# Radial layers of the second edge stage: one block-diagonal product of 512 columns instead of four 64-column products of 256

## The chip, the core and the metric

The kernel runs on one core of one Trainium2 chip. The metric is the device time of one execution, in microseconds (us). It is told as the median of several runs.

## The reference

Two graph layers are applied to 2000 nodes of 256 features, with 64000 edges sorted by their target node. The change lies in the edge part of the second layer, cut here to what matters:

```python
r = silu(edge_rbf @ M1)            # edge_rbf 64000 x 16, M1 16 x 64
r = silu(r @ M2)                   # 64 x 64
r = silu(r @ M3)                   # 64 x 64
tpw = (r @ M4).reshape(-1, 4, 64)  # 64 x 256
x0, x1 = up0[src], up1[src]
m0e = tpw[:, 0] * x0 * sh0 + tpw[:, 3] * (x1 . sh1) / sqrt(3)
m1e = tpw[:, 1] * x0 * sh1 + tpw[:, 2] * x1 * sh0
msg0, msg1 = segment_sum(m0e, dst), segment_sum(m1e, dst)
```

The first three lines are the three radial layers. Everything is in float32.

## The kernel before, in words

The program has three parts: the first layer's edge stage (to about 975 us of the trace), the second layer's edge stage (about 975 to 2050 us), and a dense end (node updates, norms, a feed-forward block). No scheduler orders the work. Each engine has its own instruction list, written out by hand, and they meet through semaphores.

The second edge stage goes over the edges in *quads* of 4 x 128 = 512 edges, 126 of them (`NQ`), and in *octets* of two quads, 63 of them (`NO`). The lists are unrolled. Per quad:

- POOL gathers 4 x 128 rows of the node table (`utab`) into `G1`, three quads deep (L423); it waits until DVE has used the slot (`s_prod`).
- PE computes `weights` (L936): the last radial product with M4, four products of 64 rows, 128 columns of weights and 256 moving columns, into banks 2 and 3. There is one such buffer, so it waits for DVE's products of the quad before.
- DVE forms the messages in three products of `weights` and the gathered rows (L1354 once, L1356 twice).
- PE sums them by target node in `segment` (L944, four products side by side of 32 weight columns and 512 moving columns, bank 4). ACT collects the bank (L580 to L582), PE turns it with five small products in `turn` (L954), and DVE adds it to the result two quads late (L1346, four times).

Per octet of 1024 edges the three radial layers run once. `layer` on PE (L923) makes the products of one layer, and `silu` on ACT (L572) applies the activation from PSUM into `R1`, `R2` or `R3`. There are 3 x 63 + 4 = 193 layers. An octet's edges lie in `RBF` and in `R1` to `R3` as two halves of 64 partitions (16 for `RBF`) by 512 columns. A layer has four products: `h` chooses the 64 rows of weights and input, `g` the 256 input columns and the 64 output partitions; output goes to bank `h`, columns 0 to 255. So each uses one quarter of the 128 x 128 array, and `two(w)` stores a layer's matrix twice, one under the other, in the same 64 columns. A float32 product stands in the trace as two records, so a layer has eight matrix records.

PE's order in one octet is: weights (second quad), layer 1, segment, [mix1], layer 2, turn, weights (first quad of the next octet), layer 0, segment, [mix1], turn. `mix1` (L968, L975) is dense work of the attention block, put in during the first 112 quads. SP loads `RBF` (L389), two DMAs of 16 rows an octet, three octets deep. A layer waits for the silu of the layer before it (`s_silu`), a silu for its layer (`s_mlp`).

Of the kernel before, what the change touches and what calls it, by code (L numbers as in the profile page):

```python
# [32 lines left out]
ACT = mybir.ActivationFunctionType  # L33
AX = mybir.AxisListType

P = 128
# [7 lines left out]
H = 64  # L44
# [19 lines left out]
RBS = ROUNDS + 1  # L64
OCT = 8 * P
# [23 lines left out]
def build(nc, A, out):  # L89
    ctx = ExitStack()  # L90
    with ctx:
# [3 lines left out]
        def sem(name):  # L95
            return ctx.enter_context(nc.semaphore(name))
# [17 lines left out]
        ps = ctx.enter_context(nc.psum_tensor("ps", [P, 8, 512], F32))  # L114
# [97 lines left out]
        m1 = a2.take(P)  # L212
        m2 = a2.take(P)
        m3 = a2.take(P)
# [21 lines left out]
        R1 = a3b.take(OCT // 2)  # L236
        R2 = a3b.take(OCT // 2)
        R3 = a3b.take(OCT // 2)
        RBF = a3b.take(3 * OCT // 2).rearrange("p (g e) -> p g e", g=3)
# [48 lines left out]
        rbl = [sem(f"rbl{k}") for k in range(3)]  # L288
# [26 lines left out]
        def _(sp):  # L315
# [66 lines left out]
            with sp.Fori(0, npass) as j:  # L382
                sp.wait_ge(S["s_mlp"], j * MLPS + 9)
                sp.sem_inc(S["s_step"], 1)
                with sp.Fori(0, RBS) as i:
                    for k in range(3):
                        sp.wait_ge(S["s_mlp"], j * MLPS + 9 * i + 3 * k + 1)
                        for h in range(2):
                            sp.dma_start(RBF[h * H:h * H + 16, k, :],  # L389
                                         A["rbf"][bass.ds((3 * i + k) * 32 + 16 * h, 16), :]).then_inc(rbl[k], 16)  # L390
                for k in range(3):
                    sp.wait_ge(rbl[k], (j + 1) * RBS * 32)
                    sp.sem_inc(S["s_step"], 1)
            sp.wait_ge(S["s_base1"], 1)
            ld(fw1.rearrange("p k c -> p (k c)"), A["fw1"], "s_fw1")
# [34 lines left out]
        def _(act):  # L430
# [138 lines left out]
            def silu(j, o, layer_):  # L569

                act.wait_ge(S["s_mlp"], j * MLPS + 3 * o + layer_ + 10)
                act.activation((R1, R2, R3)[layer_].rearrange("p (b e) -> p b e", b=2), ps[:, 0:2, 0:256],  # L572
                               ACT.Silu).then_inc(S["s_silu"], 1)

            def collect(j, n, par):

# [73 lines left out]
            for i in range(8):  # L650
                c, o = divmod(i, 2)
# [5 lines left out]
            for i in range(8):  # L657
                c, k = divmod(i, 2)
# [17 lines left out]
        def _(pe):  # L676
# [30 lines left out]
            for c in range(4):  # L707
                pe.wait_ge(S["s_lt"], 2)
                for k in range(2):
                    mm = pe.matmul(ps[0:H, c, :], w1g[:, k, :], LT[:, k, 512 * c:512 * c + 512],  # L710
                                   start=(k == 0), stop=(k == 1))
# [134 lines left out]
            with pe.Fori(0, npass) as j:  # L846
                for n in range(-3, QT + 6):
# [7 lines left out]
                    b, k = divmod(n - 8, QB)  # L855
# [10 lines left out]
            for c in range(4):  # L866
                pe.matmul(ps[half_of(c), c, 0:NCH], idd, vacc[:, c * NCH:(c + 1) * NCH],
                          start=True, stop=True).then_inc(S["s_u"], 1)
            for i in range(8):
                c, o = divmod(i, 2)  # L870
                pe.wait_ge(S["s_ue"], c + 1)
                if i >= 4:
                    pe.wait_ge(S["s_o0"], i - 3)
                pe.matmul(ps[:, 4 + i % 4, 0:NCH], w2g[half_of(c), o * P:(o + 1) * P], U[half_of(c), c * NCH:(c + 1) * NCH],
                          start=True, stop=True).then_inc(S["s_mo"], 1)
            to_rows(1)
            to_cols(1)
            for i in range(8):
                c, o = divmod(i, 2)
                pe.wait_ge(col[1], 2 * c + 2)  # L880
                pe.wait_ge(S["s_ff"], i - 3) if i >= 4 else pe.wait_ge(row[1], 8)
                for k in range(2):
                    mm = pe.matmul(ps[:, 4 + i % 4, :], wfT[:, k, o * P:(o + 1) * P], YT[:, k, 512 * c:512 * c + 512],
                                   start=(k == 0), stop=(k == 1))
# [6 lines left out]
            for i in range(NT // 2):  # L891
# [3 lines left out]
                for t in range(2):  # L895
                    for k in range(2):
                        mm = pe.matmul(ps[:, 4 + i % 4, t * D + k * P:t * D + (k + 1) * P],
                                       YT[:, k, (2 * i + t) * P:(2 * i + t + 1) * P], bu[:, k, :], start=True, stop=True)
# [11 lines left out]
            def layer(j, o, layer_, par=0, rbn=0, after=True):  # L910

                if layer_ == 0:
                    pe.wait_ge(rbl[par], (j * RBS + rbn + 1) * 32)
                    w, x, k = m1, RBF[:, par, :], 16
                else:
                    w, x, k = ((m2, R1, H), (m3, R2, H))[layer_ - 1]
                if after:
                    pe.wait_ge(S["s_silu"], j * MLPS + 3 * o + layer_)
                pe.sem_inc(S["s_step"], 1)
                for h in range(2):  # L920
                    for g in range(2):
                        hs = slice(h * H, h * H + k)
                        mm = pe.matmul(ps[g * H:(g + 1) * H, h, 0:256], w[hs, 0:H], x[hs, g * 256:(g + 1) * 256],  # L923
                                       start=True, stop=True)
                mm.then_inc(S["s_mlp"], 1)

            def weights(j, n, quad, octet):

# [64 lines left out]
            with pe.Fori(0, npass) as j:  # L993
                for layer_ in range(3):
                    layer(j, 0, layer_, after=layer_ > 0)
                layer(j, 1, 0, 1)
                weights(j, 0, 0, 0)
                for o in range(NO):
                    n = 2 * o
                    weights(j, n + 1, 1, None)  # L1000
                    layer(j, o + 1, 1)
                    segment(j, n, 0, 2 * (o % 3))
                    mix1(j, n)
                    layer(j, o + 1, 2)
                    turn(j, n - 1, 1)
                    weights(j, n + 2, 0, o + 1)
                    layer(j, o + 2, 0, (o + 2) % 3, (o + 2) // 3)
                    segment(j, n + 1, 1, 2 * (o % 3) + 1)
                    mix1(j, n + 1)
                    turn(j, n, 0)  # L1010
                pe.wait_ge(S["s_Gm1"], j + 1)
                turn(j, NQ - 1, 1)
                pe.wait_ge(S["s_silu"], (j + 1) * MLPS)
                for k in range(3):
                    pe.wait_ge(rbl[k], (j + 1) * RBS * 32)

            pe.wait_ge(S["s_base1"], 1)
            pe.wait_ge(S["s_w4"], 16 * NLOAD["s_w4"])
            for i in range(NT // 2):
                if i >= 4:  # L1020
                    pe.wait_ge(S["s_are"], i - 3)
                for t in range(2):
                    for h in range(NA):
                        mm = pe.matmul(ps[:, 4 + i % 4, t * D:(t + 1) * D], acc1[:, h, (2 * i + t) * P:(2 * i + t + 1) * P],  # L1024
                                       wl[:, h, :], start=(h == 0), stop=(h == NA - 1))
# [15 lines left out]
            for i in range(8):  # L1041
                c, o = divmod(i, 2)
                pe.wait_ge(S["s_are"], i + 5) if i < 4 else pe.wait_ge(S["s_y1e"], i - 3)
                for k in range(2):
                    mm = pe.matmul(ps[:, 4 + i % 4, :], GM1[:, k, o * P:(o + 1) * P], YT[:, k, 512 * c:512 * c + 512],
                                   start=(k == 0), stop=(k == 1))
# [3 lines left out]
            for i in range(8):  # L1050
                c, k = divmod(i, 2)
# [4 lines left out]
                          stop=True).then_inc(S["s_o"], 1)  # L1056

            pe.wait_ge(S["s_nr"], 1)
            for o in range(2):
                for k in range(2):  # L1060
                    mm = pe.matmul(ps[:, 0, o:o + 1], pat[:, k, o, :], ss[:, k:k + 1], start=(k == 0), stop=(k == 1))
# [6 lines left out]
            for c in range(4):  # L1068
                pe.wait_ge(col[3], 2 * c + 2)
                for k in range(2):  # L1070
                    mm = pe.matmul(ps[:, 4 + c, :], wrb[:, k, :], YT[:, k, 512 * c:512 * c + 512],
                                   start=(k == 0), stop=(k == 1))
# [6 lines left out]
            for i in range(32):  # L1079
# [3 lines left out]
                for k in range(2):  # L1083
                    mm = pe.matmul(ps[:, i % 4, :], fw1[:, k, m * P:(m + 1) * P], YT[:, k, 512 * c:512 * c + 512],  # L1084
                                   start=(k == 0), stop=(k == 1))
                mm.then_inc(S["s_hh"], 1)
            pe.wait_ge(S["s_wcol"], 4)
            for t in range(NT):
# [3 lines left out]
                for m in range(8):  # L1092
                    mm = pe.matmul(ps[:, 4 + t % 4, 0:D], HT[:, m, t * P:(t + 1) * P], fw2[:, m, :],  # L1093
                                   start=(m == 0), stop=(m == 7))
# [555 lines left out]
```

## Time and profile before

| | us |
|---|---|
| median of 3 runs | 1866.14 |
| lowest and highest | 1862.92, 1867.08 |
| span of the profiled execution | 2285.7 |
| first edge stage in it, with the start | 975 |
| second edge stage in it | 1075 |
| dense end in it | 236 |
| mean granted TensorE clock | 0.776 |

The profiled execution's own time is its span; nothing outside the span is recorded. It is 419.6 us longer than the median of the runs without the profiler, so its terms must be carried over with care. In the profile PE is the matrix product, PEld the loading of weights, DVE the vector engine, ACT the activation engine, POOL the engine that issues the gathers, SP the one that issues the other DMAs. "PEclk" is the granted TensorE clock; it has two levels here, 1.0 (2.4 GHz) and 0.5 (1.2 GHz).

### The profile page before, as it was taken

To read this page: it belongs to the slowest core of one execution; us is meant where nothing else is said; L and a number is where in the kernel's file an instruction comes from. 1 tells how busy PE (TensorE), PEld (TensorE's weight loads), DVE (VectorE), ACT (ScalarE), POOL (GpSimd) and SP (SyncE) were. 2 spreads that over 40 slices of the span, in tenths; PEclk is the share of its full clock that TensorE was granted. 3 is DMA by queue.
4 is the path that set the end of the run, shared out by engine and by line. 5 is a ranking of instruction groups with operands and counts; after the bars stand their busy time and mean duration, and the time that the engine had idled before them with its cause. 6 is when DMAs were issued, how large, how long until landed. Compare 5 with 4: busy or idle time off the path is not lost.

```text
span 2285.7 us, 35842 instructions
## 1 busy us (share of the span) xinstructions
PE 1697.3 (74%) x11519; PEld 981.8 (43%) x11519; DVE 951.6 (42%) x2352; ACT 654.0 (29%) x2149; POOL 956.8 (42%) x1008
## 2 busy tenths in 40 slices
PE   3567677776777765757768787878778887889699
PEld 1344344444444443523434343444334443447448
DVE  5234334433332324724434343444444434446583
ACT  2222222222222221423333233333333323222330
POOL 0656565655555551044444444444444444420000
PEclk8577787787887786867867677777777767679799
DMA  5222222222222221232222222222222222210001
GB/s 181 64 58 58 61 63 57 63 62 63 58 63 62 63 58 38 91 100 65 64 69 63 62 64 69 68 62 69 62 66 70 69 70 69 69 41 19 1 0 36
DMA packets 78941, 142.23 MB, mean 62 GB/s; under 512 B 25483, under 2 KB 33963, under 8 KB 78249
## 3 DMA queue, kind: packets, MB, share of 16 engines
q0 software_dynamic: 40128, 81.99, 14.1%
q1 hardware_dynamic: 38632, 57.99, 8.5%
q8 instruction: 96, 1.57, 0.3%
q14 instruction: 85, 0.69, 0.1%
HBM read 135.22 MB, written 4.67 MB: 61 GB/s over the span
## 4 chain that ended last, share of the span: by engine, by line
PE 43%; another core or an unknown queue 26%; DVE 13%; issue 9%; ACT 6%; DVEq 2%; DMA 1%; SPq 0%; ACTq 0%
PE ps L936 6%; PE ps L944 5%; PE ps L766 4%; PE ps L923 4%; DVE arena L1356 4%; PE ps L954 3%; PE ps L1093 2%; PE ps L1084 2%; PE ps L968 2%; DVE arena L1223 2%; PE ps L1024 2%; PE ps L793 2%; ACT wfT L587 1%; DVE arena L1354 1%
## 5 line engine op out<-in xcount | busy, mean ns | idle before, releaser
L423 POOL DMA_INDIRECT arena<-utab,src x500 | 474.1, 948 | 683.9 <-DVE arena L1356 420.2
L413 POOL DMA_INDIRECT ring<-mtab,src x500 | 480.5, 961 | 391.7 <-issue 185.5
L1223 DVE TENSOR_TENSOR arena<-ps,ring 128x1024 f32<-128x1024 f32 x125 | 153.1, 1225 | 486.8 <-ACT ring L480 232.9
L936 PE MATMUL ps<-arena 64*128 64x256 f32 x1016 | 203.1, 534 | 146.5 <-DVE arena L1356 88.9
L572 ACT ACTIVATE arena<-ps 128x512 f32<-128x512 f32 x193 | 116.7, 604 | 615.8 <-PE ps L923 353.7
L1346 DVE TENSOR_TENSOR arena<-arena,ps 128x40 f32 x512 | 100.4, 196 | 439.2 <-remote 279.7
L954 PEld LDWEIGHTS ps<-small,arena 128*128 128x128 f32 x1270 | 193.6, 234 | 94.6 <-issue 88.0
L766 PE MATMUL ps<-arena,ring 128*64 128x128 f32 x2000 | 197.9, 333 | 41.5 <-issue 41.0
L1356 DVE TENSOR_TENSOR arena<-ps,arena 128x768 f32<-128x768 f32 x252 | 228.4, 948 | 0.0
L923 PE MATMUL ps<-arena 64*64 64x256 f32 (+1 forms) x1544 | 168.3, 513 | 73.5 <-ACT arena L572 54.1
L944 PE MATMUL ps<-arena 128*32 128x512 f32 x1008 | 208.6, 842 | 10.9 <-issue 8.6
L954 PE MATMUL ps<-small,arena 128*128 128x32 f32 x1270 | 203.8, 315 | 2.3 <-DVE arena L1346 2.2
L936 PEld LDWEIGHTS ps<-arena 64*128 64x128 f32 x1016 | 118.7, 252 | 172.2 <-issue 82.7
L766 PEld LDWEIGHTS ps<-arena,ring 128*64 128x64 f32 x2000 | 145.6, 167 | 73.9 <-issue 63.9
L923 PEld LDWEIGHTS ps<-arena 64*64 64x64 f32 (+1 forms) x1544 | 49.2, 161 | 197.7 <-issue 197.0
L1354 DVE TENSOR_TENSOR arena<-ps,arena 128x512 f32<-128x512 f32 x126 | 87.2, 692 | 105.7 <-issue 41.3
L503 ACT ACTIVATE arena<-ps 128x512 f32<-128x512 f32 x125 | 75.0, 600 | 176.8 <-remote 122.4
L743 PE MATMUL ps<-small,arena 128*128 128x128 f32 x125 | 45.1, 360 | 105.1 <-DVE arena L1223 67.1
L750 PE MATMUL ps<-small,arena 128*97 128x128 f32 x125 | 53.6, 429 | 89.3 <-ACT ring L493 85.8
L1234 DVE TENSOR_TENSOR vacc<-vacc,ring 128x8 f32 x500 | 83.1, 166 | 60.4 <-DVE vacc L1234 8.5
L779 PE MATMUL ps<-arena,W2S 128*64 128x160 f32 x800 | 93.9, 348 | 4.3 <-issue 4.1
L474 ACT ACTIVATE arena<-ps,small 128x128 f32<-128x128 f32 x125 | 45.8, 367 | 165.3 <-remote 153.9
(223 smaller groups left out, 2035.7 us busy)
## 6 DMA issues: line engine op xcount, KB each, us to landing
arena<-in_eaT SPq DMA_DIRECT2D x125, 256.0 KB
ring<-mtab,src POOLq DMA_INDIRECT x500
arena<-utab,src POOLq DMA_INDIRECT x500
arena<-in_rbf SPq DMA_DIRECT2D x132, 32.0 KB
ring<-in_fw SPq DMA_DIRECT2D x2, 1024.0 KB, 5.8
utab<-arena SPq DMA_DIRECT2D x1, 2048.0 KB, 7.5
XT<-in_xT SPq DMA_DIRECT2D x2, 1000.0 KB
arena<-in_x SPq DMA_DIRECT2D x1, 1920.0 KB, 9.6
```

The source lines that it names most:

```text
L413: pool.indirect_dma_start(MR[:, n % 4, k, 0:H], None, mtab, bass.IndirectOffsetOnAxis(ap=src[:, 4 * n + k:4 * n + k + 1], axis=0)).then_in ...
L423: pool.indirect_dma_start(G1[:, n % NSLOT, k, :], None, utab, bass.IndirectOffsetOnAxis(ap=src[:, 4 * n + k:4 * n + k + 1], axis=0)).then_ ...
L572: act.activation((R1, R2, R3)[layer_].rearrange("p (b e) -> p b e", b=2), ps[:, 0:2, 0:256], ACT.Silu).then_inc(S["s_silu"], 1)
L766: mm = pe.matmul(ps[h * H:(h + 1) * H, 2 + n % 2, t * P:(t + 1) * P], MR[:, n % 4, t, 0:H], RM[:, n % 2, t, 16 * h:16 * h + 16, :].rearran ...
L923: mm = pe.matmul(ps[g * H:(g + 1) * H, h, 0:256], w[hs, 0:H], x[hs, g * 256:(g + 1) * 256], start=True, stop=True)
L936: mm = pe.matmul(ps[:, 2 + h, a * D:(a + 1) * D], R3[hs, c:c + P], m4[hs, :], start=True, stop=True)
L944: mm = pe.matmul(ps[32 * t:32 * t + 32, 4, :], SS[:, slot // 2, slot % 2 * 4 + t, :, :].rearrange("p k w -> p (k w)"), Q[:, par, t, :], st ...
L954: tr = pe.matmul(turned[:, 32 * m:32 * m + 32], EV[:, par, b:b + 2, :].rearrange("p b c -> p (b c)"), pick[:, k, :, :], start=True, stop=True)
L1223: dve.tensor_tensor(RM[:, n % 2, :, :, :], ps[:, 1, 0:P].rearrange("p (t q) -> p t q", t=4).unsqueeze(3).broadcast_to([P, 4, KH, WIN]), SW ...
L1346: dve.tensor_tensor(a, a, sums(t), ALU.add).then_inc(S["s_rmw1"], 1)
L1354: return dve.tensor_tensor(q[:, :, 0:5:4, :], tp[:, :, 0:2, :], x[:, :, 0:1, :].broadcast_to([P, 4, 2, H]), ALU.mult)
L1356: return dve.tensor_tensor(q[:, :, 4 * part - 3:4 * part, :], tp[:, :, part + 1:part + 2, :].broadcast_to([P, 4, 3, H]), x[:, :, 1:4, :], ...
```

## The change

Each layer becomes one product over the whole array with 512 moving columns. `two(w)` now puts the second copy of a matrix in the columns 64 to 127 and right below the first copy, so that the 128 x 128 matrix (32 x 128 for layer 0) is block-diagonal. The host lays `rbf` out so that one DMA of 32 rows brings an octet. The output goes to bank 0 and bank 1 in turn, by `(o + layer_) % 2`, and ACT reads one bank of 512 columns. The waits are the same, with counts adapted to one DMA in the place of two.

```diff
@@ SP
-                        for h in range(2):
-                            sp.dma_start(RBF[h * H:h * H + 16, k, :],
-                                         A["rbf"][bass.ds((3 * i + k) * 32 + 16 * h, 16), :]).then_inc(rbl[k], 16)
+                        sp.dma_start(RBF[0:32, k, :], A["rbf"][bass.ds((3 * i + k) * 32, 32), :]).then_inc(rbl[k], 16)
@@ ACT, silu
-                act.activation((R1, R2, R3)[layer_].rearrange("p (b e) -> p b e", b=2), ps[:, 0:2, 0:256],
-                               ACT.Silu).then_inc(S["s_silu"], 1)
+                act.activation((R1, R2, R3)[layer_], ps[:, (o + layer_) % 2, :], ACT.Silu).then_inc(S["s_silu"], 1)
@@ PE, layer
                 if layer_ == 0:
-                    pe.wait_ge(rbl[par], (j * RBS + rbn + 1) * 32)
-                    w, x, k = m1, RBF[:, par, :], 16
+                    pe.wait_ge(rbl[par], (j * RBS + rbn + 1) * 16)
+                    w, x = m1[0:32, :], RBF[0:32, par, :]
                 else:
-                    w, x, k = ((m2, R1, H), (m3, R2, H))[layer_ - 1]
+                    w, x = ((m2, R1), (m3, R2))[layer_ - 1]
                 if after:
                     pe.wait_ge(S["s_silu"], j * MLPS + 3 * o + layer_)
                 pe.sem_inc(S["s_step"], 1)
-                for h in range(2):
-                    for g in range(2):
-                        hs = slice(h * H, h * H + k)
-                        mm = pe.matmul(ps[g * H:(g + 1) * H, h, 0:256], w[hs, 0:H], x[hs, g * 256:(g + 1) * 256],
-                                       start=True, stop=True)
-                mm.then_inc(S["s_mlp"], 1)
+                pe.matmul(ps[:, (o + layer_) % 2, :], w, x, start=True, stop=True).then_inc(S["s_mlp"], 1)
@@ host
-    A["rbf"] = np.ascontiguousarray(rb.reshape(3 * RBS, 2, 2, 2, P, 16).transpose(0, 1, 5, 2, 3, 4).reshape(-1, OCT // 2))
+    A["rbf"] = np.ascontiguousarray(rb.reshape(3 * RBS, 2, 2, 2, P, 16).transpose(0, 2, 5, 1, 3, 4).reshape(-1, OCT // 2))
     def two(w):
         a = np.zeros((128, 128), np.float32)
         a[:w.shape[0], :64] = w
-        a[64:64 + w.shape[0], :64] = w
+        a[w.shape[0]:2 * w.shape[0], 64:] = w
         return a
```

No instruction changes its place between others. On PE, in the first octet's body of the second edge stage, the list of before reads (line, operation, output and inputs, rows x columns of the input, how many times; L936 weights, L923 layer, L944 segment, L968 mix1, L954 turn; ISA and REGISTER_ALU are waits):

```order
L936 MATMUL ps<-arena 128x256 x4
L918 REGISTER_ALU
L923 MATMUL ps<-arena 64x256 x4
L942 REGISTER_ALU
L944 MATMUL ps<-arena 32x512 x4
L964 ISA
L968 MATMUL ps<-arena 128x512 x2
L918 REGISTER_ALU
L923 MATMUL ps<-arena 64x256 x4
L952 ISA
L954 MATMUL ps<-small,arena 128x32 x5
```

and the same place after the change (L928 weights, L917 layer, L936 segment, L960 mix1, L946 turn):

```order
L928 MATMUL ps<-arena 128x256 x4
L915 REGISTER_ALU
L917 MATMUL ps<-arena 128x512
L934 REGISTER_ALU
L936 MATMUL ps<-arena 32x512 x4
L956 ISA
L960 MATMUL ps<-arena 128x512 x2
L915 REGISTER_ALU
L917 MATMUL ps<-arena 128x512
L944 ISA
L946 MATMUL ps<-small,arena 128x32 x5
```

Only the layer's rows differ: four products of 256 columns became one of 512. On SP, in the loop that loads `RBF` (L389 before, L388 after; one of its three slots shown):

```order
-L389 ISA
-L389 DMA arena<-in_rbf 16x512
-L389 ISA
-L389 DMA arena<-in_rbf 16x512
+L388 ISA
+L388 DMA arena<-in_rbf 32x512
```

One DMA of 32 rows stands where two of 16 rows stood.

## Rows read from the trace of the kernel before

**Rows 1.** The page: its head and busy line (us, share, instructions)
```profile
span 2285.7 us, 35842 instructions
...
PE 1697.3 (74%) x11519; PEld 981.8 (43%) x11519; DVE 951.6 (42%) x2352; ACT 654.0 (29%) x2149; POOL 956.8 (42%) x1008
```

**Rows 2.** By stretch: length, busy us (count) PE PEld DVE ACT POOL, PEclk, DMA share, GB/s
```profile
0.00:975.00 975.00, 642.56 (x5657) 405.27 (x5657) 374.35 (x992) 259.37 (x783) 480.70 (x504) 0.79 0.27 69
975.00:2050.00 1075.00, 849.65 (x5082) 436.11 (x5082) 441.05 (x1061) 337.43 (x1274) 476.15 (x504) 0.73 0.24 66
2050.00:2286.00 236.00, 205.09 (x782) 140.40 (x780) 136.19 (x300) 57.16 (x92) 0.00 (x0) 0.93 0.04 14
1506.00:1514.00 8.00, 7.33 (x69) 4.50 (x68) 5.56 (x11) 3.44 (x21) 3.99 (x5) 1.00 0.21 59
1545.00:1553.00 8.00, 7.76 (x28) 2.98 (x29) 3.63 (x8) 1.56 (x5) 0.68 (x1) 0.50 0.17 44
2114.50:2128.00 13.50, 13.50 (x35) 5.99 (x33) 2.73 (x2) 5.23 (x10) 0.00 (x0) 1.00 0.00 1
```

**Rows 3.** The chain of waits, whole program (by engine), then 1000 to 2040 us (by line)
```profile
PE 43%; another core or an unknown queue 26%; DVE 13%; issue 9%; ACT 6%; DVEq 2%; DMA 1%; SPq 0%; ACTq 0%
...
by line: another core or an unknown queue 22.8%; PE ps L936 13.0%; PE ps L944 11.7%; issue 8.7%; PE ps L923 8.1%; DVE arena L1356 7.9%; PE ps L954 6.6%; PE ps L968 4.4%; ACT wfT L587 2.8%; DVE arena L1354 2.6%; DVE arena L1346 1.9%; ACT L60
```

**Rows 4.** Groups of 1000 to 2040 us: name, shapes, count, busy us, mean ns, idle before
```profile
L923 PE MATMUL ps<-arena 64*64 64x256 f32 x992 | 104.1, 495 | 59.3 <-ACT arena L572 53.3 <-issue 5.9
L923 PE MATMUL ps<-arena 16*64 16x256 f32 x488 | 57.1, 549 | 0.0
...
L423 POOL DMA_INDIRECT arena<-utab,src x487 | 461.1, 947 | 570.0 <-DVE arena L1356 414.5 <-issue 155.5
L1356 DVE TENSOR_TENSOR arena<-ps,arena 128x768 f32<-128x768 f32 x246 | 222.9, 948 | 0.0
```

**Rows 5.** PE in order of time at the full clock: start us, length us, instructions
```profile
1505.95 0.66 PE L923 MATMUL ps<-arena 64*64 64x256 f32 x8
1506.54 1.30 PE L954 MATMUL ps<-small,arena 128*128 128x32 f32 x10
1508.14 1.13 PE L936 MATMUL ps<-arena 64*128 64x256 f32 x8 [0.30 <-DVE arena L1356]
1509.20 0.66 PE L923 MATMUL ps<-arena 16*64 16x256 f32 x8
1509.80 1.06 PE L944 MATMUL ps<-arena 128*32 128x512 f32 x8
1510.79 1.30 PE L954 MATMUL ps<-small,arena 128*128 128x32 f32 x10
1512.46 1.13 PE L936 MATMUL ps<-arena 64*128 64x256 f32 x8 [0.37 <-DVE arena L1356]
```

**Rows 6.** The same at the half clock
```profile
1547.25 1.13 PE L923 MATMUL ps<-arena 16*64 16x256 f32 x8
1548.31 1.94 PE L944 MATMUL ps<-arena 128*32 128x512 f32 x8
1550.17 3.78 PE L968 MATMUL ps<-arena 128*128 128x512 f32 x4
```

**Rows 7.** PE in the last stage, single products of 512 columns at the full clock
```profile
2114.59 1.02 PE L1054 MATMUL ps<-arena,ring 128*128 128x512 f32 x2
2115.45 1.02 PE L1055 MATMUL ps<-arena,ring 128*128 128x512 f32 x2
```

**Rows 8.** Waits of 1000 to 2040 us: who for whom, us in total, times, longest
```profile
DVE arena L1346 <- remote: 279.7, 39, 8.7
PE ps L936 <- DVE arena L1356: 79.4, 36, 8.4
...
SPq L389 <- PE ps L923: 740.9, 48, 21.6
```

**Rows 9.** POOL in order of time: one gather of L423
```profile
1513.78 0.94 POOL L423 DMA_INDIRECT arena<-utab,src  x1 [0.30 <-issue]

```

More of the change, by code:

```diff
@@ L387, in _ @@
                         sp.wait_ge(S["s_mlp"], j * MLPS + 9 * i + 3 * k + 1)
-                        for h in range(2):
-                            sp.dma_start(RBF[h * H:h * H + 16, k, :],
-                                         A["rbf"][bass.ds((3 * i + k) * 32 + 16 * h, 16), :]).then_inc(rbl[k], 16)
+                        sp.dma_start(RBF[0:32, k, :], A["rbf"][bass.ds((3 * i + k) * 32, 32), :]).then_inc(rbl[k], 16)
                 for k in range(3):
-                    sp.wait_ge(rbl[k], (j + 1) * RBS * 32)
+                    sp.wait_ge(rbl[k], (j + 1) * RBS * 16)
                     sp.sem_inc(S["s_step"], 1)
@@ L1014, in _ @@
                 for k in range(3):
-                    pe.wait_ge(rbl[k], (j + 1) * RBS * 32)
+                    pe.wait_ge(rbl[k], (j + 1) * RBS * 16)
             pe.wait_ge(S["s_base1"], 1)
```

## The prediction

> **What bounds the kernel now.** I read the page's head first [rows 1], then the busy time of the three stages [rows 2], the chain of waits [rows 3], the groups of the second edge stage [rows 4], PE in order of time there [rows 5, 6], and last the waits [rows 8].
>
> PE is the busiest engine: 74% of the span [rows 1], and 849.65 of 1075 us (79%) in the second edge stage, where DVE is at 441 and POOL at 476 us [rows 2]. The chain of waits says the same of the path: 43% PE over the whole program, DVE 13% [rows 3]. In the second edge stage the chain holds PE's `weights` (13.0%), `segment` (11.7%), the radial layers L923 (8.1%) and `turn` (6.6%). So a longer layer is not free by itself. The clock matters as much: the mean level is 0.73 in this stage [rows 2], about half of the time at each level. At the full level PE even waits a little for DVE in each quad (0.30 and 0.37 us) [rows 5]; at the half level it runs through without a gap [rows 6].
>
> One thing must be set aside. The recorded span is 2285.7 us, the median of the runs 1866.1. In the second edge stage DVE waited 39 times, 279.7 us in all, for a releaser that the trace doesn't show (up to 8.7 us) [rows 8], and the chain has 22.8% of "unknown queue" [rows 3]. In such a place PE's records have ended and its semaphores come several us later, several of them together. I take this as something that the recording adds. The dense end has few records of this kind (236 us, PE at the 0.93 level), so the missing 419.6 us belong to the two edge stages. Shared by length, the second one takes about 1075 - 220 = 855 us when nothing is recorded, 6.8 us a quad. Durations of single instructions are taken as they stand, and the change in us is added to the recorded span and to the median alike.
>
> **The change part by part.**
>
> *The layer on PE.* Before, the four products of a layer run side by side: eight records in 0.66 us, next instruction after 1506.54 - 1505.95 = 0.59 us [rows 5]. At the half level it is 1.13 us, and 1548.31 - 1547.25 = 1.06 us to the next [rows 6]. The new layer is one product of 512 columns, two records. The dense end has exactly this: L1054 takes 1.02 us, and the next starts after 0.86 us [rows 7], at level 1.0 [rows 2]. Between neighbours of another shape I use `segment`, which also streams 512 columns twice and lies between other shapes: 1510.79 - 1509.80 = 0.99 us to the next [rows 5], 1550.17 - 1548.31 = 1.86 us at the half level [rows 6]. So layers 0 and 1 cost +0.40 us each at the full level and +0.80 at the half. Layer 2 is followed by `turn`, which also uses the whole array, so I price it without a change of shape: 0.86 - 0.59 = +0.27 us, and 1.72 - 1.06 = +0.66 at the half level (twice 0.86; no row of its own).
>
> The Trainium skill (TensorEngine Tiling, Key Properties) says that changing the tiling mode drains TensorE. The rows show it as the 0.13 us between 0.99 and 0.86. With the drain kept behind layer 2 as well, the sum below would be 60 instead of 55 us.
>
> *What lies on the path.* The chain gives L923 8.1% of 1040 us = 84 us, of 104.1 + 57.1 = 161 us busy [rows 3, 4]. With the two levels half and half, layers 0 and 1 grow by 68 to 75% (0.99/0.59, 1.86/1.06), mean 72%; layer 2 by 46 to 62%, mean 54%; together 66%. 84 x 0.66 = **+55 us**. When nothing is recorded, the unknown waits don't cover any layer, so a little more is on the path: I take **+60 us**. Bounds: 0 if each layer is covered, 128.7 x 0.60 + 64.3 x 0.465 = +107 us if all 193 layers are on the path at mixed levels (+69 at the full level, +145 at the half).
>
> *silu.* ACT reads 512 elements of one bank instead of 2 x 256 of two, same count: 0. It starts later, since the layer ends 1.02 instead of 0.66 us after its start. Who waits is PE: `weights` needs the silu of layer 2, with `turn` (1.30 us [rows 5]) between. The silu is at hand at about 1.02 + 0.7 = 1.72 us, and `turn` ends its part at about 0.86 + 1.2 = 2.06 us, so this adds nothing; if ACT is still in the squares of the attention block, the delay passes on, which is in the upper bound. Layer 2 needs the silu of layer 1, with `segment` between: 1.72 against 1.98 us, again just covered.
>
> *Alternating banks.* Each layer still waits for the silu before it, and ACT has left the bank by then. Nothing starts earlier: 0.
>
> *DMA.* 66 instead of 132 issues, the same bytes. SP waited 740.9 us for PE's layers here [rows 8], so it is far ahead: 0 in both directions. The waits for `rbl` see the same landing.
>
> *Weights.* Eight loads a layer become two; they lie under the stream of the product before, except the first one, which is exposed in both versions: 0.
>
> Sum: +60 us, so **1926 us**; the recorded span would be 2346 us if the recording cost stayed the same. It need not: a layer leaves 4 PE records instead of 16, 2316 fewer in all, so the recorded span may grow less or even shrink. It is no measure of the result.
>
> **The rivals.**
>
> *Covered.* If a quad really takes 6.8 us at the full level, PE has room: weights 1.06, segment 0.99, turn 1.30 and one and a half layers 0.9 make 4.25 us, and with the change 4.8 us (+0.54). POOL needs 4 x (0.94 + 0.30) = 5.0 us a quad [rows 9]. Then DVE and the gathers set the pace. For it: PE's small waits for DVE [rows 5], 79.4 us of them in the stage [rows 8]. Against it: the attention block's products (1.02 us a product at best) fill 112 of 126 quads up, and half the time the level is 0.5. It gives 0 to +15 us, 1866 to 1881.
>
> *All on the path.* PE's list is strictly in order, and at the half level it has no gap [rows 6]. If PE sets the pace throughout, the price is +107 us (1973), and up to +145 us (2011) if the clock stays low.
>
> *Faster, by the clock.* The level is 0.5 for half of this stage and 1.0 through the dense end, where PE streams 512 columns without a pause [rows 2, 7]. PE's list now has longer streams and fewer small pieces. If that keeps the level up, all its work gets shorter. PE's work is 0.79 x 855 = 675 us at a mean level of 0.73; at 0.85 it would take 675 x (1 - 0.73/0.85) = 95 us less, against some +50 for the layers: 1821 us. It decides from a mean level of 0.80 in this stage (675 x (1 - 0.73/0.80) = 59). Against it: the low level comes after pauses of PE, and a longer layer closes few of them; PE's share goes only from 79 to about 84%. The Trainium skill (TensorE: Matmul & The Clock Gate, The HAM clock gate) says that the gate opens by how busy PE has been recently; by that rule this rival would be the outcome if the stage is near the edge, and no row shows how near it is.
>
> *Not what it says.* If the four products did not run side by side, one product would save time. The rows rule it out: eight records of 256 columns in 0.66 us, less than one product of 512 columns (1.02 us).
>
> **How the numbers follow.** About 0.2%, 3.7 us, is what a measurement of this kernel can tell from no change. Forecast (PE's path carries about half of the layers, 1895 to 1955): 0.56. All on the path (1955 to 2011): 0.16. Covered (1866 to 1881): 0.13, of which 0.06 within 0.2%. Faster by the clock (1790 to 1862): 0.15. The range takes in the forecast, the covered case, the lower part of the path case and the edge of the clock case: 1850 to 1985, which leaves out about 0.12 below and 0.06 above. Likeliest case alone: 1895 to 1955. Faster 0.15, same 0.06, slower 0.79.
>
> **What would show it.** The profile after has 386 layer records with a mean near 600 to 1000 ns, starts 0.43 (full) or 0.85 us (half) apart, and 0.86 to 0.99 us at the full level until the next group. L923's 8% of the chain should become 12% or more. PE's waits for DVE should shrink; ACT's silu stays at 0.60 us. I am wrong if PEclk in this stage rises above 0.80, if PE's waits for DVE grow while the quad keeps its length, or if `weights` starts to wait for ACT's silu.

## The result and the profile after

The changed kernel takes 1902.36 us (median of 4 runs, 1901.39 to 1903.58), the kernel before 1866.19 us beside it: ratio 1.0206, 95% interval 1.0194 to 1.0219. It is 36 us slower. 1926 us was forecast, so the direction was right and the size two thirds too large. One execution of the kernel before, beside three of the later runs, took 3185.71 us and is left out of their ratios.

These lines are from the page of the profile of the kernel after (span, busy time, clock by slice, chain by engine and by line, two groups; L917 is the layer, L928 is `weights`):

```profile
span 1901.8 us, 33328 instructions
...
PE 1560.5 (82%) x10361; PEld 906.0 (48%) x10361; DVE 953.4 (50%) x2352; ACT 667.5 (35%) x2149; POOL 956.0 (50%) x1008
...
PEclk9688888989888878697978888888888888998899
...
PE 55%; POOL 12%; issue 11%; DVE 9%; ACT 5%; DMA 5%; DVEq 1%; SPq 0%; POOLq 0%; ACTq 0%; PEldq 0%
POOL ring L411 12%; PE ps L917 10%; PE ps L928 8%; PE ps L936 7%; PE ps L946 5%; DMA ring<-mtab,src 4%; PE ps L960 3%; DVE arena L1348 3%; PE ps L763 3%; PE ps L1085 3%; PE ps L1076 3%; PE ps L1016 2%; PE ps L776 2%; PE ps L695 1%; ACT wfT 
...
L917 PE MATMUL ps<-arena 128*128 128x512 f32 (+1 forms) x386 | 248.7, 729 | 13.3 <-DMA arena<-in_rbf 10.9
L928 PE MATMUL ps<-arena 64*128 64x256 f32 x1016 | 174.8, 471 | 92.4 <-DVE arena L1348 71.6
```

and its busy time by stage (length, busy us and count of PE, PEld, DVE, ACT, POOL, PEclk, DMA share, GB/s):

```profile
0.00:780.00 780.00, 566.82 (x5657) 366.17 (x5657) 374.64 (x992) 269.47 (x783) 479.36 (x504) 0.86 0.33 87
780.00:1667.00 887.00, 789.36 (x3940) 399.42 (x3940) 443.18 (x1063) 341.30 (x1275) 476.66 (x504) 0.86 0.28 80
1667.00:1902.00 235.00, 204.28 (x768) 140.41 (x764) 135.58 (x297) 56.73 (x92) 0.00 (x0) 0.93 0.04 14
```

The span is 1901.8 us, the same as the runs: this recording carries no waits of its own, unlike the one of before [rows 1, 8]. The two can't be set side by side, so the kernel before was recorded again, as the first experiment.

PE in order of time in the kernel after, around a change of the clock:

```profile
1080.46 1.12 PE L917 MATMUL ps<-arena 128*128 128x512 f32 x2
1081.51 1.06 PE L936 MATMUL ps<-arena 128*32 128x512 f32 x8
1082.51 1.13 PE L917 MATMUL ps<-arena 128*128 128x512 f32 x2
1083.47 1.20 PE L946 MATMUL ps<-small,arena 128*128 128x32 f32 x10
1088.35 2.08 PE L928 MATMUL ps<-arena 64*128 64x256 f32 x8 [3.68 <-DVE arena L1348]
1090.36 2.07 PE L917 MATMUL ps<-arena 32*128 32x512 f32 x2
1092.35 1.94 PE L936 MATMUL ps<-arena 128*32 128x512 f32 x8
...
1102.15 1.98 PE L960 MATMUL ps<-arena 128*128 128x512 f32 x4
1103.97 1.02 PE L917 MATMUL ps<-arena 128*128 128x512 f32 x2
1104.83 0.42 PE L946 MATMUL ps<-small,arena 128*128 128x32 f32 x3
```

A layer 0 or 1 takes 1.12 us, and the next group starts after 1.05 us at the full level (1080.46 to 1081.51); at the half level it is 2.07 and 1.99 us (1090.36 to 1092.35). Layer 2 ahead of `turn` takes 0.96 us (1082.51 to 1083.47), or 0.86 behind `mix1` (1103.97 to 1104.83). These rows answer to [rows 5, 6]. One pause of 3.68 us stands in them too, where `weights` waits for DVE.

### The profile page after: what moved, and what is told of

Its sections match the earlier page's. It is cut to its first block, busy times and chain, and to the rows that moved or that the text cites. A ratio compares the mean times of both kernels' runs of the same rounds, so it can differ in the third digit from the quotient of the medians.

```text
span 1901.8 us, 33328 instructions
## 1 busy us (share of the span) xinstructions
PE 1560.5 (82%) x10361; PEld 906.0 (48%) x10361; DVE 953.4 (50%) x2352; ACT 667.5 (35%) x2149; POOL 956.0 (50%) x1008
## 4 chain that ended last, share of the span: by engine, by line
PE 55%; POOL 12%; issue 11%; DVE 9%; ACT 5%; DMA 5%; DVEq 1%; SPq 0%; POOLq 0%; ACTq 0%; PEldq 0%
POOL ring L411 12%; PE ps L917 10%; PE ps L928 8%; PE ps L936 7%; PE ps L946 5%; DMA ring<-mtab,src 4%; PE ps L960 3%; DVE arena L1348 3%; PE ps L763 3%; PE ps L1085 3%; PE ps L1076 3%; PE ps L1016 2%; PE ps L776 2%; PE ps L695 1%; ACT wfT L584 1%
## 5 line engine op out<-in xcount | busy, mean ns | idle before, releaser
L917 PE MATMUL ps<-arena 128*128 128x512 f32 (+1 forms) x386 | 248.7, 729 | 13.3 <-DMA arena<-in_rbf 10.9
L928 PE MATMUL ps<-arena 64*128 64x256 f32 x1016 | 174.8, 471 | 92.4 <-DVE arena L1348 71.6
L946 PEld LDWEIGHTS ps<-small,arena 128*128 128x128 f32 x1270 | 168.5, 203 | 80.2 <-issue 78.5
L946 PE MATMUL ps<-small,arena 128*128 128x32 f32 x1270 | 166.9, 281 | 1.5 <-DVE arena L1338 1.5
L763 PE MATMUL ps<-arena,ring 128*64 128x128 f32 x2000 | 164.0, 315 | 0.0
L936 PE MATMUL ps<-arena 128*32 128x512 f32 x1008 | 159.3, 709 | 0.0
L754 PE MATMUL ps<-ring 128*32 128x97 f32 x1000 | 50.7, 277 | 131.0 <-DMA ring<-mtab,src 130.3
L928 PEld LDWEIGHTS ps<-arena 64*128 64x128 f32 x1016 | 103.5, 220 | 113.5 <-DVE arena L1348 45.6
L917 PEld LDWEIGHTS ps<-arena 128*128 128x128 f32 (+1 forms) x386 | 66.1, 210 | 117.1 <-issue 117.1
L754 PEld LDWEIGHTS ps<-ring 128*32 128x32 f32 x1000 | 25.7, 116 | 153.9 <-issue 79.2
L577 ACT ACTIVATE arena<-ps 128x256 f32<-128x256 f32 x126 | 48.3, 383 | 89.4 <-PE ps L936 89.4
```

The lines of the kernel that those rows point to most:

```text
L763: mm = pe.matmul(ps[h * H:(h + 1) * H, 2 + n % 2, t * P:(t + 1) * P], MR[:, n % 4, t, 0:H], RM[:, n % 2, t, 16 * h:16 * h + 16, :].rearran ...
L917: pe.matmul(ps[:, (o + layer_) % 2, :], w, x, start=True, stop=True).then_inc(S["s_mlp"], 1)
L928: mm = pe.matmul(ps[:, 2 + h, a * D:(a + 1) * D], R3[hs, c:c + P], m4[hs, :], start=True, stop=True)
L936: mm = pe.matmul(ps[32 * t:32 * t + 32, 4, :], SS[:, slot // 2, slot % 2 * 4 + t, :, :].rearrange("p k w -> p (k w)"), Q[:, par, t, :], st ...
L946: tr = pe.matmul(turned[:, 32 * m:32 * m + 32], EV[:, par, b:b + 2, :].rearrange("p b c -> p (b c)"), pick[:, k, :, :], start=True, stop=True)
```

## The experiments

All are compared with the kernel before on the same chip, and their medians stand in one table at the end of this section. The stage columns are of each run's own profile, from 785 us to the end of the last `turn` of the second edge stage; the rows shown with single runs stop 3 to 12 us before that, which can change a level by 0.01. "Level" is the mean granted TensorE clock of a stretch, as a share of the full 2.4 GHz; it is made up of stretches at 1.0 and at 0.5.

**The kernel before, recorded again.** No edit.

> The kernel before, unchanged, recorded once more. Theory 1 (PE's list sets the pace of the second edge stage, and the longer stream is what costs): the recording of before carried waits of its own (semaphores that came late); without them the second edge stage lasts about 850 us, PE is busy 75 to 80% of it, L923 holds about 8 to 10% of the chain, and the mean clock of the stage is about that of the changed kernel. Theory 2 (the clock paid part of the cost back): the stage of before shows a mean clock clearly below that of the changed kernel, by 0.03 or more. Theory 3 (the late semaphores belong to the kernel, not to the recording): they show again, and the span is again far above the median. Time: 1866 us in all cases.

1863.6 us, ratio 0.9997 (0.9987 to 1.0007). Its page, then its stages:

```profile
span 1861.9 us, 35842 instructions
...
PE 1509.2 (81%) x11519; PEld 889.3 (48%) x11519; DVE 951.8 (51%) x2352; ACT 666.3 (36%) x2149; POOL 956.6 (51%) x1008
...
PEclk9698989988889877787878778888887887988999
...
PE 51%; POOL 16%; issue 12%; DVE 9%; ACT 6%; DMA 4%; DVEq 1%; SPq 0%; POOLq 0%; ACTq 0%; PEldq 0%
```

```profile
0.00:780.00 780.00, 568.10 (x5657) 363.68 (x5657) 374.81 (x992) 269.67 (x783) 480.75 (x504) 0.86 0.32 87
780.00:1628.00 848.00, 737.47 (x5108) 385.27 (x5108) 441.49 (x1063) 340.73 (x1278) 475.89 (x504) 0.82 0.30 84
1628.00:1862.00 234.00, 203.60 (x754) 140.39 (x754) 135.53 (x297) 55.92 (x88) 0.00 (x0) 0.92 0.04 14
```

The late semaphores are gone and the span is 1861.9 us, so theory 3 falls: they belonged to that recording. The second edge stage (780 to 1628 us) lasts 848 us; it is 887 in the kernel after. The other two stages are equal within 1 us. PE was already busy for 87% of this stage, where theory 1 had 75 to 80%. The chain by line of this kernel (800 to 1600 us), then of the kernel after (800 to 1640 us):

```profile
by line: PE ps L936 18.8%; PE ps L944 18.1%; PE ps L923 12.5%; PE ps L954 11.6%; PE ps L968 9.1%; DVE arena L1356 6.4%; issue 4.2%; ACT wfT L587 3.1%; ACT L605 2.3%; ACT ring L610 1.7%; ACT arena L572 1.4%; DVE arena L1354 1.4%; ACT arena L
```

```profile
by line: PE ps L917 20.4%; PE ps L928 17.4%; PE ps L936 15.9%; PE ps L946 10.1%; PE ps L960 7.9%; DVE arena L1348 6.1%; issue 4.7%; ACT wfT L584 2.7%; ACT ring L607 1.5%; ACT L602 1.4%; DVE arena L1346 1.4%; ACT arena L570 1.3%; ACT arena L
```

The layers go from 12.5% (L923; theory 1 had 8 to 10%) to 20.4% (L917) of the chain. And the mean clock level of the stage rises from 0.82 to 0.86, as theory 2 had it.

**One bank.** The changed kernel with `ps[:, 0, :]` in `layer` and `silu`.

```diff
-                act.activation((R1, R2, R3)[layer_], ps[:, (o + layer_) % 2, :], ACT.Silu).then_inc(S["s_silu"], 1)
+                act.activation((R1, R2, R3)[layer_], ps[:, 0, :], ACT.Silu).then_inc(S["s_silu"], 1)
...
-                pe.matmul(ps[:, (o + layer_) % 2, :], w, x, start=True, stop=True).then_inc(S["s_mlp"], 1)
+                pe.matmul(ps[:, 0, :], w, x, start=True, stop=True).then_inc(S["s_mlp"], 1)
```

> The changed kernel, with all layers writing bank 0. Theory 1 and 2: the alternation does nothing, since each layer waits for the silu before it: 1902 us, within 0.1%. Rival (alternating banks hide part of the cost, since ACT's read and PE's next write no longer meet in one bank): 5 us or more above 1902.

1900.91 us, ratio 1.0189 (1.0169 to 1.0210). The alternation is worth nothing.

**Full array twice.** The changed kernel with each product issued twice.

```diff
+                pe.matmul(ps[:, (o + layer_) % 2, :], w, x, start=True, stop=True)
                 pe.matmul(ps[:, (o + layer_) % 2, :], w, x, start=True, stop=True).then_inc(S["s_mlp"], 1)
```

> The changed kernel, with each layer's product issued twice into the same bank. One more product of 512 columns adds 0.86 us at the full clock and 1.72 at the half, without a new change of shape. 193 of them are 166 us at the full clock. Theory 1 (PE sets the pace): 120 us or more above 1902, since whatever room PE had is used up. Theory 2 (clock): the mean clock rises and the step is under 100 us. Rival (only a part of the stage is paced by PE, the rest by gathers and DVE): a step of some 60 to 110 us with an unchanged clock.

2017.78 us, 115 us above the changed kernel, just short of the 120 of theory 1 and above the 100 of theory 2. Both were half right, and the rival's unchanged clock did not show: PE's idle time in the stage shrank by 29 us and the level rose to 0.90:

```profile
785.00:1775.00 990.00, 924.11 (x4287) 465.66 (x4289) 438.00 (x1051) 338.92 (x1270) 472.12 (x502) 0.90 0.25 71
```

**Quarters twice.** The kernel before with its four products issued twice.

```diff
-                for h in range(2):
+                for h in (0, 1, 0, 1):
```

> The kernel before, with each layer's four products issued twice. It streams as many columns per layer as the changed kernel (2 x 2 x 256 instead of 2 x 512), in quarters of the array, with the same neighbours and 32 records per layer instead of 16 and 4. Theory 1: +0.43 us of stream per layer, so 1900 to 1910 us, like the changed kernel; the difference to 1902 is what the shape of layer 2 and its drain are worth (at most 5 us). Rival (the cost lies in the full-array form itself, its 128-column weight loads or its longer way through the array, not in the stream): under 1885 us. Rival (issue of instructions matters): above 1915 us.

1905.57 us, ratio 1.0218 (1.0200 to 1.0236), within 4 us of the changed kernel and inside the forecast. The cost follows the length of the stream. Neither rival shows: not the full-array form with its 128-column weights, and not the number of instructions (6634 matrix records in its stage against 3938):

```profile
785.00:1668.00 883.00, 793.42 (x6634) 439.83 (x6634) 441.44 (x1057) 341.30 (x1274) 473.52 (x502) 0.86 0.28 80
```

**Layer 0 alone.** Layer 0 as in the changed kernel, layers 1 and 2 in quarters. PE's part of the edit, cut; `silu` and the host's matrices follow it.

```diff
+                if layer_ == 0:
+                    mm = pe.matmul(ps[:, 0, :], m1[0:32, :], RBF[0:32, par, :], start=True, stop=True)
+                else:
...
+                    for h in range(2):
+                        for g in range(2):
```

> Layer 0 as in the changed kernel, layers 1 and 2 in quarters as before. By the distances in the clean traces at the full level a layer of the changed kernel costs +0.46 us (layers 0 and 1) or +0.27 us (layer 2, with what it saves in front of turn), 1.19 us an octet, for 36 us measured. If each layer counts by its own price, this one costs 0.46/1.19 of it: +14 us, 1878 us. If the cost comes from layers 1 and 2 alone (the ones behind a silu that PE waits for): 1864 us. If it comes from layer 0 alone: 1900 us.

1899.83 us, ratio 1.0191 (1.0174 to 1.0208): a third of the added stream cost the whole 36 us. The forecast that goes price by price (1878 us) was wrong, and the 1900 us of "layer 0 alone" came out. The stage's row shows where the time went:

```profile
785.00:1668.00 883.00, 782.70 (x4709) 395.64 (x4708) 441.09 (x1057) 339.95 (x1275) 473.23 (x502) 0.81 0.28 80
```

PE is busy as long as in the changed kernel, with less work, at a level of 0.81 in place of 0.86. So the time is not the price of layer 0, and the last experiment bears that out.

**Filler in the pauses.** In the clean recording of before, one of PE's long waits looks like this (ACT and DVE, then PE):

```profile
880.80 1.28 ACT L605 ACT_TABLE_LOAD   x1
882.09 0.21 ACT L605 ACTIVATE arena<-arena 128x8 f32<-128x8 f32 x1
882.32 1.28 ACT L572 ACT_TABLE_LOAD   x1
882.33 0.20 DVE L1374 RECIPROCAL arena<-arena 128x8 f32<-128x8 f32 x1 [5.82 <-ACT arena L605]
...
885.62 1.36 PEld L936 LDWEIGHTS ps<-arena 64*128 64x128 f32 x8 [3.48 <-issue]
885.62 2.08 PE L936 MATMUL ps<-arena 64*128 64x256 f32 x8 [3.38 <-DVE arena L1356]
```

DVE waits 5.82 us with its reciprocal (for the attention block) until ACT's square root is done, which sits between two loads of activation tables of 1.28 us each. DVE's products of the quad come behind it, so PE's `weights` waits 3.38 us. This comes 16 times. The filler puts six products that nobody reads in front of that wait, in the changed kernel on one bank:

```diff
             def weights(j, n, quad, octet):
+                if n and n % 7 == 0 and n <= 7 * NT:
+                    for _ in range(6):
+                        pe.matmul(ps[:, 1, 0:256], ident, YT[:, 0, 0:256], start=True, stop=True)
                 pe.wait_ge(S["s_prod"], j * NQ + n + 3)
```

> The changed kernel on one bank, with six products of 256 columns into the free bank 1 ahead of each of PE's 16 long pauses (in front of weights, where it waits for DVE 3.7 to 4.5 us). At the full clock they take 2.6 us and fit into the pause. Clock theory: the level no longer falls behind the pause, the mean level rises above 0.86 and the time falls by 5 to 40 us below 1901, though PE does more. Rival (the level falls for another reason, or doesn't matter): 1901 us or above.

1834.46 us, 66 us below the same kernel without filler. More work on PE made it faster, by more than the 5 to 40 us expected. The stage, and the end of one filler (L923) with the wait behind it:

```profile
785.00:1604.00 819.00, 767.19 (x4127) 408.83 (x4130) 440.59 (x1057) 341.36 (x1275) 472.55 (x501) 0.94 0.30 86
```

```profile
835.78 1.03 PE L923 MATMUL ps<-arena,small 128*128 128x256 f32 x4
838.62 1.13 PE L931 MATMUL ps<-arena 64*128 64x256 f32 x8 [1.82 <-DVE arena L1351]
839.69 1.12 PE L917 MATMUL ps<-arena 128*128 128x512 f32 x2
```

The level is 0.94, and `weights` runs at the full level behind the pause (1.13 us), where it ran at the half level before (2.08 us in the rows above). The filler adds 46 us of work and takes up 44 us of idle time; what makes the stage 61 us shorter is that PE is busy at the half level for 89 us in place of 214 (the table below). So the clock, and not only the list of PE, sets this stage's time.

**The same filler with quarters.** Into bank 0, behind the wait for the silu.

```diff
-                pe.wait_ge(S["s_prod"], j * NQ + n + 3)
                 if octet is not None:
                     pe.wait_ge(S["s_silu"], j * MLPS + 3 * octet + 3)
+                if n and n % 7 == 0 and n <= 7 * NT:
+                    if octet is None:
+                        pe.wait_ge(S["s_silu"], j * MLPS + 3 * (n // 2 + 1) + 1)
+                    for _ in range(6):
+                        pe.matmul(ps[:, 0, 0:256], ident, YT[:, 0, 0:256], start=True, stop=True)
+                pe.wait_ge(S["s_prod"], j * NQ + n + 3)
```

> The kernel before with the same six products of 256 columns in front of weights in each of the 16 long pauses, here into bank 0 after the silu of the layer before. In the changed kernel the filler took 66 us off and raised the stage's level from 0.86 to 0.94. Clock theory: the kernel before gains at least as much, since its level is lower (0.82): 1790 to 1810 us, level 0.90 or more, and the difference to the changed kernel with filler (1834) stays 25 us or more. Rival (the filler helped only the full-array form): 1864 us or above.

1832.29 us, ratio 0.9851 (0.9811 to 0.9890). It gains 32 us, not 55 to 75, and the difference between the forms, forecast at 25 us or more, is 2 us, which is within the spread of these runs (1824 to 1842 and 1833 to 1841 us). The profiled execution is the fastest of them here (1824.43) and the slowest with the filler in the full array (1841.27), so their stages are 17 us apart. The level is 0.90, against 0.94 there. Here the filler stands behind one more wait, and PE waits in front of it 8 times for the silu:

```profile
PE ps L935 <- ACT arena L572: 20.7, 8, 2.6
```

Whether that is why the level stays lower was not tried.

**The reciprocal one quad later,** with quarters and with the full array.

```diff
-                    if t < NT and f == 5:
+                    if t < NT and f == 6:
                         dve.wait_ge(S["s_v1std"], c + 1)
```

> The kernel before, with DVE's reciprocal for the attention block (L1374) one quad later. In the clean recording of before, DVE waits there 16 times for ACT's square root (68.7 us in all), and PE then waits 3.4 to 4.5 us for DVE each time. If these pauses are PE's only large room, most of them go: 1864 less 30 to 60 us. If ACT's wait for the reciprocal takes their place, under 10 us are gained. Clock theory: with the pauses gone, the mean level of the stage rises above the 0.82 of before, to 0.86 or more.

> The changed kernel with the same later reciprocal. Clock theory (in the plain pair the changed kernel got back about half of its longer stream because its level is 0.86 against 0.82): with the pauses gone both are nearer to the full level, the payback gets smaller, and the difference between this run and the one with quarters grows from 36 to 50 us or more. Theory that the cost was covered by PE's room in the pauses: it grows too, by no more than the idle time that the change used up (11 us). Neither: it stays at 36 us.

1801.73 us (ratio 0.9676, 0.9660 to 0.9692) and 1835.54 us (0.9861, 0.9831 to 0.9890). The first is 62 us faster, where 30 to 60 were forecast. The pauses above 3 us go and the levels are 0.86 and 0.89. But the two differ by 34 us, as the plain pair does. The forecast of 50 us or more was wrong: what clock and idle time give back stayed as large at a higher level.

**The silu of layer 2 ahead of the attention work,** on top of the last edit, again in both forms.

```diff
                     collect(j, 2 * o, 0)
-                    mix1(j, 2 * o)
                     silu(j, o + 1, 2)
+                    mix1(j, 2 * o)
```

> The kernel before with the later reciprocal (1802 us), and ACT's silu of layer 2 ahead of the attention block's work in each octet. In late_recip_quarters PE waits 46.2 us in all for that silu. If they go, 1802 less 20 to 60 us (the waits, and what the level gains); if the attention block's later work takes their place, 1802 us or above.

> The same two edits with the changed kernel's layers. PE then has few pauses, and the level can rise by little. A layer costs +0.46 or +0.27 us at the full level, 77 us in all. Clock theory: the nearer both are to the full level, the more of the 77 us is seen: 45 us or more between this run and the one with quarters. It was 34 us with the later reciprocal alone; if it stays there, the payback does not come from how near the level is to full.

1697.56 us (ratio 0.9112, 0.9091 to 0.9134) and 1739.75 us (0.9329, 0.9308 to 0.9350). Their stages, quarters first:

```profile
785.00:1458.00 673.00, 635.24 (x5090) 345.80 (x5085) 436.93 (x1057) 339.00 (x1274) 473.99 (x503) 0.96 0.37 105
```

```profile
785.00:1505.00 720.00, 697.83 (x3950) 366.07 (x3949) 440.12 (x1058) 345.00 (x1278) 474.85 (x503) 0.98 0.34 98
```

The levels are 0.96 and 0.98. The version with quarters gained 104 us on the last edit, where 20 to 60 were forecast, and lies 167 us below the kernel before. The difference between the forms is 42 us. That is short of the 45 that the clock theory asked for and above the 34 of the last pair, but each difference is known to about 6 us only, so it decides neither.

**Layer 0 alone, near the full level.** The same with layer 0 only in the full-array form.

> silu_first_quarters (1698 us) with layer 0 alone as in the changed kernel. In layer0_full, with the pauses in place, this cost 36 us, as much as all three layers, at a stage level of 0.80 to 0.81. Clock theory: that was the clock falling more often, not the layer; here the level stays near 0.96, and the layer costs its own part of the 42 us between silu_first_quarters and silu_first_full, 0.46/1.19 of it: 16 us, 1714 us (1707 to 1722). Rival (layer 0's form itself is dear, its 32-row weights or its place ahead of segment): 1735 us or more.

1702.83 us (1693.05 to 1706.17), ratio 0.9129 (0.9103 to 0.9154): 5 us above the same kernel with quarters, and the two intervals overlap. That is less than the 16 expected, and far from the 36 that it cost with the pauses in place. The form of layer 0 is not dear.

```profile
785.00:1464.00 679.00, 652.50 (x4704) 348.27 (x4708) 441.54 (x1061) 340.02 (x1275) 475.30 (x504) 0.98 0.36 104
```

All runs together. "At half" is the part of PE's busy time in which the level is 0.5, summed over these stretches of the trace. "Work" is PE's busy time less half of that, an estimate of the time that its products would take at the full level.

| kernel | us | stage | PE busy | at half | PE idle | level | work |
|---|---|---|---|---|---|---|---|
| before, recorded again | 1863.6 | 847 | 740 | 269 | 107 | 0.82 | 605 |
| changed | 1902.4 | 886 | 790 | 223 | 96 | 0.86 | 679 |
| one bank | 1900.9 | 885 | 787 | 214 | 98 | 0.86 | 680 |
| quarters twice | 1905.6 | 889 | 798 | 215 | 91 | 0.86 | 690 |
| full array twice | 2017.8 | 1002 | 935 | 178 | 67 | 0.90 | 846 |
| layer 0 alone | 1899.8 | 887 | 785 | 301 | 102 | 0.81 | 635 |
| filler, full array | 1834.5 | 824 | 771 | 89 | 53 | 0.94 | 726 |
| filler, quarters | 1832.3 | 807 | 729 | 151 | 78 | 0.90 | 653 |
| late reciprocal, quarters | 1801.7 | 781 | 711 | 207 | 70 | 0.86 | 608 |
| late reciprocal, full | 1835.5 | 816 | 763 | 163 | 52 | 0.90 | 681 |
| silu first, quarters | 1697.6 | 679 | 640 | 55 | 39 | 0.95 | 612 |
| silu first, layer 0 | 1702.8 | 685 | 657 | 25 | 28 | 0.98 | 644 |
| silu first, full | 1739.8 | 723 | 700 | 32 | 23 | 0.97 | 684 |

A stage is its work, plus half of "at half", plus the idle time. The work hardly depends on the rest: 605 to 612 us for plain quarters, 679 to 684 with the full array, and 29 to 32 us more for layer 0 alone (64 x 0.46 = 29 by the price of one layer at the full level); the filler's own products come to 46 to 48 us. The quarters twice add 85 us (193 x 0.43 = 83, since each of their products starts 0.43 us after the last), and the change adds 74. (A group takes about 1.87 times as long at the half level, not twice: `segment` 1.87 against 1.00 us in the rows above. With this the added work is 71 to 72 us in all three pairs.) What the change costs depends on what the other two columns give back (differences to the same kernel with quarters, rounded):

| pair | work | half level | idle | stage |
|---|---|---|---|---|
| plain | +74 | -23 | -11 | +40 |
| late reciprocal | +74 | -22 | -17 | +34 |
| silu first | +72 | -12 | -16 | +44 |
| layer 0 alone, plain | +30 | +16 | -5 | +40 |
| layer 0 alone, silu first | +32 | -15 | -11 | +6 |

## Why the prediction was right in direction and too large

- *What bounds the kernel: right.* PE sets the pace of the second edge stage, and the long waits of [rows 8] were the recording's. The stage was put at 855 us; it is 848.
- *The layer on PE: nearly right.* Layers 0 and 1 cost 1.05 - 0.59 = +0.46 us at the full level (forecast +0.40) and 1.99 - 1.06 = +0.93 at the half (forecast +0.80): a full-array layer between other shapes takes a little longer than `segment`, from which the price came. Layer 2 behind `segment` costs 0.96 - 0.59 = +0.37, but `turn` behind it starts `weights` 0.10 us sooner (the shortest distance is 1.13 instead of 1.23 us), so +0.27 as forecast. That holds for 38 of the 63 octets. In the other 25 `mix1` stands in front of layer 2; there the layer costs 0.86 - 0.59 = +0.27, `turn` gives back its 0.10, and `mix1` starts the layer 0.10 us sooner (1103.97 - 1102.15 = 1.82 us in the rows of the kernel after, 1102.98 - 1101.06 = 1.92 us in these of the kernel before). So only +0.07 is left:

```profile
1101.06 1.99 PE L968 MATMUL ps<-arena 128*128 128x512 f32 x4
1102.98 0.66 PE L923 MATMUL ps<-arena 64*64 64x256 f32 x8
```

  At the full level this gives 128.7 x 0.46 + 38 x 0.27 + 25 x 0.07 = 71 us, in agreement with the 71 to 74 us of the tables. The Trainium skill (TensorEngine Tiling, Key Properties) says that changing the tiling mode drains TensorE. The rows agree: a full-array layer takes 1.05 us between other shapes and 0.86 behind and before the same shape.
- *What lies on the path: the step that failed.* The sum took half of the layers (84 of 161 us on the chain), at a clock that the change leaves alone. Both halves of this were off. Nearly all of the added stream is on the path: PE has 74 us more work, and its idle time fell by only 11. But the clock does not stay: PE was busy at the half level for 223 us in place of 269, which gave back 23. 74 - 11 - 23 = 40 us, and the stage grew by 40. The forecast of 60 came as near as it did by two errors of opposite sign, which is luck.
- *The rival "faster, by the clock": the mechanism was right, the size not.* The level rose, from 0.82 to 0.86, and not by enough. Its turning point of 0.80 was read from the disturbed recording and meant nothing: the clean level of before is already 0.82. The filler shows that the mechanism is real, as it shortened the time by 66 us with only products added. The Trainium skill (TensorE: Matmul & The Clock Gate, The HAM clock gate) says that the gate goes by how busy PE has been recently. The filler agrees (level 0.86 to 0.94). Layer 0 alone is not explained by it as it stands: PE is busy for 785 of 887 us (89%) in place of 740 of 847 (87%), and the level falls from 0.82 to 0.81.
- *The rival "covered": wrong.* There is no room for a layer except in the pauses. *"All on the path": right about the path.* Its 107 us took the two levels half and half, from the disturbed recording; in the clean one PE is busy at the half level for 269 of 740 us. The rest of the gap is what clock and idle time give back.
- *silu, banks, DMA, weights at 0: nothing speaks against it.* `one_bank` shows it for the banks; the waits of PE for ACT's silu did not grow (23.9 us before, 20.6 after), and PE waits for `RBF` only once, at the start (11.4 us before, 10.9 after). No run changes the loads of weights alone. These rows are of the kernel after:

```profile
PE ps L928 <- DVE arena L1348: 71.6, 30, 4.5
PE ps L928 <- ACT arena L570: 20.6, 24, 1.0
```

- *What would show it.* The layers' share of the stage's chain is 20.4%, above the 12% asked for; but it was 12.5% in the clean recording of before already, so the mark of 8% to 12% was the disturbed recording's. PE's waits for DVE fell from 78.6 to 71.6 us, as foretold. The first of the three signs of being wrong did show: PEclk in the stage is 0.86, above 0.80. It was read from the same recording. The recorded span shrank, as warned, though because the late semaphores did not come again and not by the number of records: they were missing from the second recording of before as well.

Open: which pauses make the level fall, and why layer 0 alone drops it to 0.81 while all three layers raise it to 0.86. The traces show this much. In the stage of before the level falls 36 times, 16 of them in or right behind the 16 pauses of over 3 us; in the changed kernel it falls 24 times, again 16 of them there. So the change removed falls away from the long pauses. With layer 0 alone it falls 32 times but stays low for longer, 341 us in all against 297 before and 249 in the changed kernel. With the filler (full array) no pause of over 3 us is left, and it falls 10 times. That this is the clock and not PE's work is shown by the tables; no run here shows the rule.

## What to carry to other kernels

Four products that use a quarter of the array each and run side by side were not a loss to be repaired here: one full-array product with zero blocks streams twice the columns, and costs about what issuing the quarters twice costs. Where TensorE sets the pace, count its work at the full level, its idle time and its time at the half level apart, for a change can move all three in different directions. Before shortening its work, look for the waits that make it pause: two edits of one line each in other engines' lists were worth 167 us here, more than four times what this change cost. Only 68 us of it were PE's idle time; 107 us came from PE's products running at the full level instead of the half.

## What the hardware did that was not expected

- Adding 96 products that nobody reads made the kernel 66 us faster (1900.9 to 1834.5 us), since the mean granted clock of the stage went from 0.86 to 0.94.
- A third of the change (layer 0) cost as much as all of it (36 against 36 us), at a level of 0.81, and only 5 us, not clear of noise, at a level of 0.98.
- One recording of the same kernel was 420 us longer than its runs (2285.7 against 1866), with semaphores of PE that came up to 8 us late; its edge stages took 975 and 1075 us [rows 2] instead of 780 and 848. The next recording of it had none of this (1861.9 us).
